# Gated cross attention with a feed-forward net on one core: in the even steps the turn of the maxima stands behind the fourth part of the product with V

## The reference, cut to what matters

```
xn   = layernorm(x)                                   # 112 x 256
q, k, v = xn @ wq + bq, ctx @ wk + bk, ctx @ wv + bv  # 16 heads of 16 columns
p    = softmax(q_h k_h^T / 4) for each head h         # 112 x 375
x    = x + tanh(g_xattn) * (concat_h(p v_h) @ wo + bo)
x2n  = layernorm(x)
w    = sum of the two normalised top-2 router probabilities of x2n @ router_w
x    = x + tanh(g_ffn) * (gelu(x2n @ w1 + b1) @ w2 + b2) * w
```

## Time and profile before

| | |
|---|---|
| median of 3 runs | 711.1 us (710.85 to 716.75) |
| the profiled execution | 713.49 us |
| its span, first to last instruction | 711.6 us |
| TensorE matmuls busy | 687.7 us, 97% |
| TensorE weight loads busy | 654.3 us, 92% |
| VectorE / ScalarE / GpSimd busy | 71% / 55% / 47% |
| mean granted TensorE clock | 0.99 |

### The profile page before, as it was taken

How to read it: one execution, slowest core, us unless ns; L and a number is a source line. 1 busy time by engine, 2 the same in 40 slices (tenths; PEclk the granted TensorE clock), 3 DMA queues, 4 the chain that set the end, 5 groups by cost and what they waited for, 6 DMA issues and landing times.

```text
span 711.6 us, 20678 instructions
## 1 busy us (share of the span) xinstructions
PE 687.7 (97%) x7648; PEld 654.3 (92%) x7648; DVE 506.2 (71%) x1297; ACT 394.0 (55%) x797; POOL 332.0 (47%) x478
## 2 busy tenths in 40 slices
PE   4699999999999999999999999999999999999997
PEld 3678898999999999999999999999999999988897
DVE  5588678686877868687786768778676777756534
ACT  3126666464655647465564746556474655647552
POOL 4555464354463626446362644636264463423264
PEclk9789999999999999999999999999999999999999
DMA  7666755244453525445342454624254462320000
GB/s 220 163 182 178 187 146 136 67 133 127 115 137 98 128 70 134 128 115 154 81 117 78 124 141 109 160 80 124 71 134 130 109 160 78 92 56 6 3 15 27
DMA packets 47797, 80.27 MB, mean 113 GB/s; under 512 B 10997, under 2 KB 30802, under 8 KB 47698
## 3 DMA queue, kind: packets, MB, share of 16 engines
q1 hardware_dynamic: 47378, 78.18, 41.3%
q10 hardware_dynamic: 320, 0.77, 0.3%
HBM read 30.49 MB, written 11.01 MB: 58 GB/s over the span
## 4 chain that ended last, share of the span: by engine, by line
PE 91%; DVE 3%; POOL 2%; SPq 1%; issue 1%; ACT 1%; DMA 1%; POOLq 0%; DVEq 0%; ACTq 0%
PE P L943 44%; PE S L972 13%; PE T L984 12%; PE OT L1002 11%; PE P L1028 4%; PE TR L1011 2%; PE TR L1087 1%; SPq L430 1%; DVE NEGM L781 1%; PE TR L1055 1%; PE TR L1018 1%; PE TR L1070 1%; DMA CTRAW<-in_ctxT 1%; PE TR L958 1%; DVE XN L847 1%
## 5 line engine op out<-in xcount | busy, mean ns | idle before, releaser
L781 DVE TENSOR_REDUCE NEGM<-S 112x1 f32<-112x375 f32 x512 | 267.5, 541 | 55.9 <-PE S L972 55.0
L701 ACT ACTIVATE PROBS<-T 125x448 f32<-125x448 f32 x384 | 194.6, 541 | 92.6 <-PE T L984 91.2
L972 PE MATMUL S<-KS,QS 96*112 96x376 f32 x512 | 176.5, 358 | 3.6 <-DVE NEGM L781 3.3
L984 PE MATMUL T<-QS,KS 98*125 98x224 f32 x768 | 146.9, 281 | 0.1
L984 PEld LDWEIGHTS T<-QS,KS 98*125 98x125 f32 x768 | 126.0, 188 | 4.9 <-ACT PROBS L701 1.6
L606 POOL CAST HT_HI<-HG 128x224 fp32r<-128x224 f32 x124 | 46.5, 375 | 132.9 <-ACT HG L727 132.7
L972 PEld LDWEIGHTS S<-KS,QS 96*112 96x112 f32 x512 | 88.5, 178 | 14.8 <-DVE NEGM L781 8.4
L608 POOL TENSOR_TENSOR HT_LO<-HG,HT_HI 128x224 fp32r<-128x224 f32 x124 | 82.8, 668 | 9.9
L1002 PE MATMUL OT<-PROBS,VA 125*17 125x112 f32 x3072 | 84.7, 260 | 0.0
L727 ACT ACTIVATE HG<-P,B 128x224 f32<-128x224 f32 x128 | 57.1, 448 | 48.6 <-PE P L943 47.4
L1002 PEld LDWEIGHTS OT<-PROBS,VA 125*17 125x17 f32 x3072 | 70.2, 97 | 5.9 <-issue 1.1
(11 more groups left out here) (111 smaller groups left out, 1491.4 us busy)
## 6 DMA issues: line engine op xcount, KB each, us to landing
KS<-KHI SPq DMA_DIRECT2D x124, 188.0 KB
KS<-KLO SPq DMA_DIRECT2D x128, 94.0 KB, 2.7
CTRAW<-in_ctxT SPq DMA_DIRECT2D x32, 375.0 KB, 3.3
QS<-q_parts SPq DMA_DIRECT2D x96, 112.0 KB, 3.1
X<-in_x SPq DMA_DIRECT2D x16, 224.0 KB, 3.8
q_parts<-QHI SPq DMA_DIRECT2D x32, 112.0 KB, 2.3
q_parts<-QLO SPq DMA_DIRECT2D x32, 112.0 KB, 2.3
out_y<-X SPq DMA_DIRECT2D x16, 224.0 KB, 3.4
```

What stands on the lines that cost most here:

```text
L701: act.activation(PT[0:KN, k, pp * 4 * SQ:(pp + 1) * 4 * SQ], T_BANK[i % 2][0:KN, 0:4 * SQ], ACT.Exp, scale=SCALE).then_inc(exp_done, 1)
L781: dve.tensor_reduce(NEGM[:, b.par, col:col + 1], S_BANK[i % 2][0:SQ, 0:SK], AX.X, ALU.max, negate=True).then_inc(max_done, 1)
L972: pe.matmul(S_BANK[i % 2][0:SQ, 0:SKP], QS[0:96, b.gpar, i % 2, i // 2, b.j * SQ:(b.j + 1) * SQ], KS[0:96, b.ring, i // 2, :], start=True, ...
L984: mm = pe.matmul(T_BANK[i % 2][0:KN, r * 2 * SQ:(r + 1) * 2 * SQ], KS[0:98, prv.ring, pair, k * KN:(k + 1) * KN], QS[0:98, prv.gpar, :, pa ...
```

## The change

In the list of the even steps, `mt` is taken from between `pv.2+1` and `cl+1` and put behind `pv.3+1`. Nothing else differs.

```
--- before.py
+++ after.py
@@ -71,7 +71,7 @@
 ORDER = [stages(text) for text in (
     """st.5+1 dh.0+2 s.11+1 n2+1 dn.0+2 st.6+1 wo+1 x2n+2 st.7+1 s.12+1 st.8+1 dh.1+2 st.9+1 dn.1+2 kd.0+1
        x2t s.13+1 st.10+1 s.14+1 kd.1+1 ql+1 k.0 k.1 s.15+1 st.11+1 lo.0 rt pv.0+1 pv.1+1 xn rx rw.0 rw.1
-       pv.2+1 mt cl+1 pv.3+1 rw.2 rw.3 s.0 up.0 m s.1 up.1 s.2 up.2 lo.1 s.3 au+1 up.3 s.4 up.4 lo.2 s.5
+       pv.2+1 cl+1 pv.3+1 mt rw.2 rw.3 s.0 up.0 m s.1 up.1 s.2 up.2 lo.1 s.3 au+1 up.3 s.4 up.4 lo.2 s.5
        kd.0 up.5 s.6 lo.3 lo.4 up.6 s.7 xl n1 ct s.8 up.7 s.9 v.2+1 ct-1 st.0 s.10 st.1 kd.1 s.11 rw.4 v.0
        s.12 lo.5 xt s.13 v.1 cl st.2 s.14 st.3 v.2 lo.6 rw.5 st.4 s.15 ol+1 rw.6 q.0 st.5 s.0-1 st.6 q.1""",
```

## The result

Over 20 runs each the median went from 711.92 us (710.45 to 719.69) to 715.74 us (712.33 to 721.47). The ratio of the two is 1.0047, 95% interval [1.0026, 1.0069]: slower by 1.9 to 4.9 us, 3.3 at its middle. The mean granted clock of the executions does not tell the two apart: 0.9895 and 0.9903 in two sets of the kernel after (20 and 10), 0.9910 and 0.9895 in two of the kernel before (33 and 31). The ratios of the experiments leave out two executions well above the others, one of e1 at 1323.46 us and one of e4 at 722.32.

What follows compares the result with a forecast made beforehand. TensorE bounds the kernel; per even step 0.305 us saved against a 0.58 us wait leaves 0.275, less 0.07 given back, 0.205; times 13, +2.7 us on 711.1 gives 713.8 us, range 709.0 to 716.5.

Steps and rivals of the forecast that it cites:

- What TensorE saves: TensorE around the even step's turn: one pause fewer, so the first up.0 matmul starts 0.305 us earlier, 4.0 us over 13 steps.
- Who waits for the turn: ScalarE's MHI copy, table load and HG follow the turn 0.575 us later; up.2 waits 0.58, net +0.205 us per even step.
- What else gets late: Later work on VectorE, GpSimd and SP behind the turn, all costed at nothing because other waits or slack hide it.
- HG 6: ScalarE's HG number 6, waiting for GpSimd's fourth split: slips about 0.13 us, hidden ahead of v.2+1; 1.7 us if not.
- the shift: The 0.205 us by which each even step's later work moves back; it puts HG number 6 at 311.90.
- The slip of 0.05 at `s.2`: TensorE's s.2 waits 0.05 us for VectorE's later first maximum, hidden inside the wait at up.2; otherwise 0.7 us in all.
- The loads of the maxima: SP's two loads of the maxima into QS go out 0.57 us later, over 7 us ahead of their first reader; no cost.
- The faster one: Rival at TensorE's up.2 weight load: no wait comes about, the saved pause is kept, 3.3 us faster, 707.8 us; chance 0.12.
- the link that the prediction named as the one that can't shrink: ScalarE's in-order queue of MHI, table load (1.28 us) and HG: none can shrink, and the chain comes 0.58 us too late.

Runs made afterwards that it cites:

- e1: Kernel after with GELU replaced by the identity with the same bias, so no table load stands ahead of HG; period of two steps 41.244 us, ratio 0.9925.
- e4: Kernel before with the same early one-column GELU and later router operations as e3, the turn staying ahead of part 3; period 41.590 us, ratio 1.0013.
- e3: Kernel after with a one-column GELU behind the even step's last exp, loading the table early, and the router's exp and small operations later; period 41.279 us, ratio 0.9959.
- e7: Kernel after with a one-column GELU directly behind the router's exp, which stays in place; period 41.538 us, ratio 0.9987.
- b0: Kernel before, unchanged, profiled a second time to check the clock in step 30; part of that step's product with V ran at half clock.
- e5: Kernel after with the turn one stage later still, behind s.0; period 42.030 us, ratio 1.008.

## Why the prediction was right

**What TensorE saves** was right: the first `up.0` matmul starts 0.28 behind the turn (308.01 to 308.29) as special step 4 had shown, and e1 gives 41.555 - 41.244 = 0.311 a step where I had 0.305. Seen against e4, e3 gives 0.311 too.

**Who waits for the turn** was right in place and size: turn to `up.2` 2.36 us against the forecast 2.37, a wait charged to HG 13 times, HG 0.02 behind the table load. The idle shows as 0.51 and not 0.58 mainly because it is counted from the end of the load of `s.2` (309.87), which overlaps what would have followed. Forecast 0.205 a step, measured 0.214 (0.207 without the late table load of step 16); 2.7 us forecast, 2.8 in the trace, 3.3 [1.9, 4.9] in the runs.

**What else gets late.** HG 6 slips behind GpSimd as said. I put it at 0.13 over the shift, though 311.98 against 311.90 gives 0.08; the 0.13 comes out only with the 0.05 of signalling that I added at `s.2`. It starts at 314.84, where the earlier trace rows with 0.575 and the shift lead to 307.435 + 7.05 + 0.205 = 314.69, so 0.15:

```profile
314.84 0.45 ACT L727 ACTIVATE HG<-P,B 128x224 f32<-128x224 f32 x1 [0.54 <-POOL HT_LO L608]
```

`v.2+1` comes at 316.12 and hides it. The slip of 0.05 at `s.2` did not come: the load at 309.69 is 1.40 behind the first `up.0` matmul, as before (305.80 to 307.19, 1.39). The first maximum starts 0.08 ahead of the end of the operation before it (309.04 against 308.96 + 0.16 = 309.12), which I had left out, here and in e7. The loads of the maxima cost nothing, as said: the waits of `st` (L984) for exp are 7 with 1.6 us in both kernels, and none for a load appears.

**The rivals.** The faster one, that the wait at `up.2` would not come about, is false for this change and true for e1 and e3, where the chain is shortened by just the link that the prediction named as the one that can't shrink. The prediction priced it at 3.3 us; e3's ratio gives 2.9. The Trainium skill, "TensorEngine Tiling (Array Packing)", Key Properties, says that a change of the tiling mode drains TensorE: one pause of 0.18 went with the change in every even step, so the trace agrees, and the rule alone did not tell the sign. The Trainium skill, "ScalarE: Activation LUTs", What ACT_TABLE_LOAD costs, says that a drain of 1.38 us comes on top of the load: in the kernel after the load ends last and HG starts 309.88 - 308.56 = 1.32 us behind the end of MHI, so there is no room for it; the measurement decides against it here.

**What I had no row for** is the clock in step 30. Its fall does not need the change (b0), and whether the change makes it more frequent stays open; but it and the start-up (the turn of step 6 stood at 138.41, 134.54 and 142.77 in three profiles of the kernel before) make up more of the profiled difference than the change.

## What to carry to other kernels

When a producer is moved back to save time on the engine that is the bound, follow its result through the other engines' queues to the next point where the bound engine waits for them; what counts is the slack there (0.30 us here), not the busy share of the engine between (55%). A table load stands in its queue behind whatever came before it, so an early small activation that calls for the table, placed in that engine's idle time, can take it off such a chain. And look for a place in the same trace that already has the new order: special step 4 gave both the saving and the price.

## What was not expected of the hardware

After an idle of 1.44 us of the weight loads (1.18 of the matmuls), TensorE's granted clock fell to 1.2 GHz (half) for 3 to 3.5 us in 9 of 14 profiles, beginning 1.0 to 2.3 us after the idle ended, mostly during the OT matmuls. It cost 1.5 to 1.8 us each time, an estimate from the distance between the turns of steps 28 and 31 and what it is without the fall (54.37 in the kernel before, 55.91 in b0); where part of the slow stretch lies behind the turn of step 30, less of it shows there (0.8 in b0). The same work without such an idle, in the 12 other regular even steps, ran at full clock. The waits of 0.5 and 0.7 us at `up.2` in the kernel after and in e5 were followed by no fall in those 12 steps. That this idle brings the fall is an inference from where it stands: no run took it away, and five profiles have it without the fall.
